# Layer 0's mixture: one spread gate for all row blocks, gate products on GpSimd, a token-major down-projection

## The reference, cut to what matters

```
scores = softmax(xf @ w_router.T)                 # 8 experts
expert_weights, expert_indices = top_k(scores, 2)
h = silu(einsum('td,edh->eth', xf, w1)) * einsum('td,edh->eth', xf, w3)
y = einsum('eth,ehd->etd', h, w2)
out = sum over the two chosen experts of expert_weights * y
```

## Time and profile before

| | |
|---|---|
| median of 3 runs | 1944.31 us (1942.88 to 1944.59) |
| the profiled execution | 1944.38 us, its span 1942.6 us |
| TensorE, matmuls | 1829.6 us busy, 94% |
| TensorE, weight loads | 1357.4 us, 70% |
| VectorE (DVE) | 1313.6 us, 68% |
| ScalarE (ACT) | 1128.7 us, 58% |
| GpSimd (POOL) | 1164.2 us, 60% |

### The profile page before, as it was taken

How to read it: one execution, slowest core, us unless ns; L and a number is a source line. 1 busy time by engine, 2 the same in 40 slices (tenths; PEclk the granted TensorE clock), 3 DMA queues, 4 the chain that set the end, 5 groups by cost and what they waited for, 6 DMA issues and landing times.

```text
span 1942.6 us, 32012 instructions
## 1 busy us (share of the span) xinstructions
PE 1829.6 (94%) x10178; PEld 1357.4 (70%) x10178; DVE 1313.6 (68%) x4504; ACT 1128.7 (58%) x2734; POOL 1164.2 (60%) x1702
## 2 busy tenths in 40 slices
PE   5999999998999999999999999999998999898987
PEld 3767777665666666566666667777788976796864
DVE  5964465788688777878688656435657655768673
ACT  5342344565685777667876786446445556435455
POOL 5420002479889888988898884126438655555554
PEclk9999999999999999999999999999999999899989
DMA  8000000001000000000000000000000011000001
GB/s 282 12 12 1 1 1 1 1 1 44 1 1 1 1 1 1 1 1 1 1 1 1 1 9 5 1 1 8 2 3 1 1 30 31 2 2 1 2 12 55
DMA packets 26492, 26.00 MB, mean 13 GB/s; under 512 B 3108, under 2 KB 23724, under 8 KB 25940
## 3 DMA queue, kind: packets, MB, share of 16 engines
q1 hardware_dynamic: 26324, 23.95, 4.0%
HBM read 21.80 MB, written 2.15 MB: 12 GB/s over the span
## 4 chain that ended last, share of the span: by engine, by line
PE 66%; POOL 16%; DVE 7%; ACT 6%; issue 4%; DMA 0%; POOLq 0%; SPq 0%; ACTq 0%; DVEq 0%
PE ps L86 60%; POOL arena L103 14%; PE ps L89 6%; ACT arena L97 5%; DVE arena L103 3%; ACT L97 1%; POOL arena L106 1%; DVE arena L106 1%; DVE arena L126 1%; DVE arena L109 1%; DVE arena L123 1%; DVE arena L141 1%; DMA rows<-in_rows 0%; DVE arena L129 0%; DVE arena L112 0%
## 5 line engine op out<-in xcount | busy, mean ns | idle before, releaser
L103 POOL TENSOR_TENSOR arena<-arena 128x128 f32<-128x128 f32 (+6 forms) x708 | 623.3, 891 | 298.0 <-DVE arena L109 158.6
L97 ACT ACTIVATE arena<-ps 128x128 f32<-128x128 f32 (+10 forms) x1100 | 363.3, 365 | 422.3 <-PE ps L86 305.8
L86 PE MATMUL ps<-arena 128*128 128x128 f32 (+4 forms) x2864 | 466.3, 298 | 27.1 <-DVE arena L103 12.6
L86 PEld LDWEIGHTS ps<-arena 128*128 128x128 f32 x2864 | 386.2, 194 | 125.0 <-issue 60.6
L103 DVE TENSOR_TENSOR arena<-ps,arena 128x128 f32<-128x128 f32 (+4 forms) x672 | 295.5, 450 | 173.7 <-PE ps L86 158.0
L86 PE MATMUL ps<-arena,moe 128*128 128x256 f32 (+1 forms) x1312 | 384.6, 433 | 0.7 <-DVE arena L103 0.4
L97 ACT ACTIVATE arena<-arena 128x128 f32<-128x128 f32 (+2 forms) x772 | 299.2, 438 | 59.1 <-POOL arena L103 46.1
L97 ACT ACTIVATE arena<-ps,cols 128x512 f32<-128x512 f32 x324 | 218.2, 689 | 170.0 <-PE ps L86 156.1
L86 PE MATMUL ps<-arena,cst 128*128 128x360 f32 (+1 forms) x768 | 295.5, 497 | 10.2 <-POOL arena L103 6.2
L86 PEld LDWEIGHTS ps<-arena,moe 128*128 128x128 f32 x1312 | 238.6, 192 | 69.6 <-issue 34.2
L89 PE MATMUL ps<-cst,arena 128*128 128x128 f32 (+2 forms) x1420 | 252.7, 280 | 33.2 <-ACT arena L97 17.1
(11 more groups left out here) (110 smaller groups left out, 2094.6 us busy)
## 6 DMA issues: line engine op xcount, KB each, us to landing
rows<-in_rows SPq DMA_DIRECT2D x1, 2253.0 KB, 9.2
moe<-in_L_ffn_w SPq DMA_DIRECT2D x3, 704.0 KB, 9.9
arena<-in_x SPq DMA_DIRECT2D x4, 512.0 KB, 9.0
wf<-in_wf SPq DMA_DIRECT2D x2, 1024.0 KB, 10.2
arena<-in_L_ffn_W SPq DMA_DIRECT2D x8, 256.0 KB, 3.0
out_dram<-arena SPq DMA_DIRECT2D x4, 512.0 KB, 3.2
wmod<-in_wmod SPq DMA_DIRECT2D x4, 384.0 KB, 8.8
arena<-kept SPq DMA_DIRECT2D x8, 192.0 KB, 3.0
```

Of the source, the lines that this page charges most:

```text
L86: return UNSENT if self.e is None else self.e.matmul(out, lhsT, rhs, start=start, stop=stop)
L97: return self.e.activation(out, in_, func, bias=bias, scale=scale)
L103: return UNSENT if self.e is None else self.e.tensor_tensor(out, a, c, op)
```

## The change

The units get another order: block j (of 11) holds units 16 j to 16 j + 15 of every expert, so every block has the same pattern of experts, partition p belonging to expert p // 16. `sel` shrinks to 24 x 128, and one product with it gives gates that fit all 11 blocks. The gate chain runs once for all 8 tiles. `ms` is taken twice per element (512 tokens each) and copied to SBUF by ScalarE (`gb`). The product with the gates moves to GpSimd (`mgated`). SiLU and product work in place in `hid`. `m2` has a 128-token slice of `hid` stationary and `w2` moving, 22 products a group, so its output is token-major: no `moT`, no `mo`; DVE multiplies it by the gain row, GpSimd adds it to x. The gain row of layer 0 is loaded into the place of layer 1's, which is loaded once an element's GpSimd has left the mixture. The weights are laid out on the host. All four strings of `TURNS` are new from the first hundred digits to the last.

```diff
@@ class Moe0
-        self.xn, self.hT = r.take(256), r.take(256)
-        self.hid = r.take(self.nb * 256)
-        self.sl = r.take(512)
...
+        self.hT, self.hid, self.gb = r.take(1024), r.take(self.nb * 256), r.take(1024)
+        self.xn, self.gTb = self.hid[:, 0:1024], self.hid[:, 2304:2816].bitcast(BF16)
...
@@ def moe0_pe(b)
+            for h in range(2):
+                ps = banks.take(pe, b, b, "mx", h)
...
+            for t in range(NT):
+                pe.wait_ge(*at("mh", b, t // 4))
+                ins = pe.mm(ps[:, 8 * t:8 * t + 8], m.hT[:, 128 * t:128 * t + 128], wsm("wr0"))
+            ins.then_inc(*pe.up(b, "mr", b))
+            yield
             for g in range(4):
...
-                    ps = banks.take(pe, b, b, "ms", l, g, j)
-                    pe.wait_ge(*at("mgT", b, l, g))
-                    for i in range(n):
-                        ins = pe.mm(ps[:, 256 * i:256 * i + 256], sel[:, col4(j + i)], m.gTb[0:24, :])
-                    ins.then_inc(*pe.up(b, "ms", b, l, g, j))
...
+                    if g == 0 and j == 4:
+                        yield
+                        ps = banks.take(pe, b, b, "mg")
...
+                        for t in range(NT):
+                            ins = pe.tr(pb[:, 128 * t:128 * t + 128],
+                                        m.g24[:, t, :, :].rearrange("p k e -> p (k e)"), ibf)
+                        ins.then_inc(*pe.up(b, "mg", b))
+                    if g == 0 and j == 6:
+                        for h in range(2):
...
+                            pe.mm(ps[:, :], sel[:, :], m.gTb[0:24, 512 * h:512 * h + 512]).then_inc(
+                                *pe.up(b, "ms", b, h))
...
-                pe.wait_ge(*at("mhid", b, l, g))
-                for j in range(m.nb):
-                    ins = pe.mm(ps[:, 0:256], w2[:, j, :], m.hid[:, 256 * j:256 * j + 256], start=(j == 0),
-                                stop=(j == m.nb - 1))
-                ins.then_inc(*pe.up(b, "m2", b, l, g))
...
-                for i in range(2):
-                    ins = pe.tr(ps[:, col4(i)], m.xn[:, col4(i)], ident)
-                ins.then_inc(*pe.up(b, "mo", b, l, g))
+                pe.wait_ge(*at("mgated", b, g))
                 for i in range(2):
+                    for j in range(m.nb):
+                        at_hid = 256 * j + 128 * i
+                        ins = pe.mm(ps[:, col4(i)], m.hid[:, at_hid:at_hid + 128], w2[:, j, :], start=(j == 0),
+                                    stop=(j == m.nb - 1))
+                ins.then_inc(*pe.up(b, "m2", b, g))
...
@@ def moe0_act(b)
+                    act.wait_ge(*at("m1", b, g, j))
+                    if g:
+                        act.wait_ge(*at("m2", b, g - 1))
+                    act.act(m.part(j, n), ps[:, 0:256 * n], ACT.Silu).then_inc(
+                        *act.up(b, "m1x", b, g, j, free=(b, "m1", g, j)))
...
+                            act.act(m.gb[:, 512 * h:512 * h + 512], ps[:, :]).then_inc(
+                                *act.up(b, "mgb", b, h, free=(b, "ms", h)))
...
@@ def moe0_dve(b)
-                    dve.tt(hj, hj, ps[:, 0:256 * n], ALU.mult).then_inc(*dve.up(b, "mhid", b, l, g, free=(b, "ms", l, g, j)))
...
+                dve.tt(four(m.group(g)), four(ps[:, 0:256]), over(r.row(5), 2), ALU.mult).then_inc(
+                    *dve.up(b, "my", b, g, free=(b, "m2", g)))
...
@@ def moe0_pool(b)
+                for j, n in moe_pairs(m.nb):
+                    yield
+                    hj = m.part(j, n).rearrange("p (j t) -> p j t", t=256)
+                    pool.wait_ge(*at("mgb", b, g // 2))
+                    pool.wait_ge(*at("mprod", b, g, j))
+                    pool.tt(hj, hj, over(m.gb[:, 256 * g:256 * g + 256], n), ALU.mult).then_inc(
+                        *pool.up(b, "mgated", b, g))
+                yield
+                xg = r.x[:, 2 * g:2 * g + 2, :]
+                pool.wait_ge(*at("my", b, g))
+                pool.tt(xg, xg, four(m.group(g)), ALU.add).then_inc(*pool.up(b))
...
@@ def queue_first(), SyncE
+            load("m1", moe0[0], A["w1f0"])
+            load("m3", moe0[1], A["w3f0"])
+            load("m2", moe0[2], A["w2f0"])
+            for b in range(B):
+                spread(f"gain0_{b}", b, 0, 5, 6)
...
                 queue_rows(b, 1, "l0", "dve")
-                spread(f"gain1_{b}", b, 1, 5, 6)
             queue_mods(2)
             queue_mods(3)
+            for b in range(B):
+                queue_gain(b, 1, ("moe", 0))
             queue_moe1()
...
@@ def constants()
-    sel = (r[:, None] == (np.arange(1408)[None, :] // 176)) * np.uint16(0x3F80)
+    sel = (r[:, None] == (i[None, :] // 16)) * np.uint16(0x3F80)
```

More of the change, by code:

```diff
@@ new lines, in moe0_pe @@
+            w2 = four(moe0[2])
+            enter(pe, b, "l0")
+            for h in range(2):
+                ps = banks.take(pe, b, b, "mx", h)
+                pe.wait_ge(*at("mn", b, h))
+                for i in range(4):
+                    ins = pe.tr(ps[:, col4(i)], m.tile(4 * h + i), ident)
+                ins.then_inc(*pe.up(b, "mx", b, h))
+                yield
+            ps = banks.take(pe, b, b, "mr")
+            for t in range(NT):
+                pe.wait_ge(*at("mh", b, t // 4))
+                ins = pe.mm(ps[:, 8 * t:8 * t + 8], m.hT[:, 128 * t:128 * t + 128], wsm("wr0"))
@@ new lines, in moe0_act @@
+            enter(act, b, "l0")
+            for h in range(2):
+                act.wait_ge(*at("mstats", b, h))
+                for t in range(4 * h, 4 * h + 4):
+                    norm_act(b, m.tile(t), r.x[:, t, :], t, "mn", b, h)
+                yield
+            for h in range(2):
+                ps = banks.get(b, "mx", h)
+                act.wait_ge(*at("mx", b, h))
+                act.act(m.hT[:, 512 * h:512 * h + 512], ps[:, :], scale=mcol(0, 4, b), bias=mcol(0, 3, b)).then_inc(
+                    *act.up(b, "mh", b, h, free=(b, "mx", h)))
+                yield
@@ new lines, in moe0_act @@
+                    act.act(m.part(j, n), ps[:, 0:256 * n], ACT.Silu).then_inc(
+                        *act.up(b, "m1x", b, g, j, free=(b, "m1", g, j)))
+                    if g == 0 and j == 2:
+                        yield
+                        act.wait_ge(*at("mshift", b))
+                        act.act(m.pr, m.pr, ACT.Exp).then_inc(*act.up(b, "mexp", b))
+                    if g == 0 and j == 4:
+                        yield
+                        ps = banks.get(b, "mg")
+                        act.wait_ge(*at("mg", b))
+                        act.act(m.gTb[0:24, :], ps[0:24, :].bitcast(BF16)).then_inc(
+                            *act.up(b, "mgT", b, free=(b, "mg")))
@@ L977, in moe0_dve @@
+                    if g == 0 and j == 6:
+                        for h in range(2):
+                            yield
+                            ps = banks.get(b, "ms", h)
+                            act.wait_ge(*at("ms", b, h))
+                            act.act(m.gb[:, 512 * h:512 * h + 512], ps[:, :]).then_inc(
+                                *act.up(b, "mgb", b, h, free=(b, "ms", h)))
+                yield
+            leave(act, b, ("moe", 0))
         def moe0_dve(b):
-            l, after = 0, "l0"
@@ L979, in moe0_dve @@
             m, r = Moe0(room[b]), room[b]
-            enter(dve, b, after)
-            yield from stats(b, [(r.x[:, t, :], t) for t in range(NT)])
-            yield from scales(b, "mstats", b, l)
+            enter(dve, b, "l0")
+            for h in range(2):
+                yield from stats(b, [(r.x[:, t, :], t) for t in range(4 * h, 4 * h + 4)])
+                yield from scales(b, "mstats", b, h)
+            yield
+            ps = banks.get(b, "mr")
+            dve.wait_ge(*at("mr", b))
@@ new lines, in moe0_dve @@
+            dve.cp(m.lg, ps[:, 0:64].rearrange("p (t e) -> p t e", e=8)).then_inc(*dve.up(b, free=(b, "mr")))
+            yield
+            dve.wait_ge(*dve.last(b))
+            for t in range(NT):
+                dve.max8(m.mx[:, t, :], m.lg[:, t, :]).then_inc(*dve.up(b))
+            yield
+            dve.wait_ge(*dve.last(b))
+            dve.tt(m.pr, m.lg, m.mx[:, :, 0:1].broadcast_to([128, NT, 8]), ALU.subtract).then_inc(
+                *dve.up(b, "mshift", b))
+            for t in range(NT):
+                dve.max_index(m.ix[:, t, :].bitcast(U32), m.mx[:, t, :], m.lg[:, t, :]).then_inc(*dve.up(b))
@@ L1053, in moe0_dve @@
[L1053 to L1059 removed]
+                for j, n in moe_pairs(m.nb):
+                    yield
+                    ps = banks.get(b, "m3", g, j)
+                    dve.wait_ge(*at("m3", b, g, j))
+                    dve.wait_ge(*at("m1x", b, g, j))
+                    dve.tt(m.part(j, n), ps[:, 0:256 * n], m.part(j, n), ALU.mult).then_inc(
+                        *dve.up(b, "mprod", b, g, j, free=(b, "m3", g, j)))
```

463 lines of the change are left out of this document (182 added, 281 removed).

## The result

The changed kernel takes 1882.45 us (median of 4 runs, 1881.73 to 1883.93) where the kernel before, run beside it, takes 1944.45 (1942.88 to 1946.16): a ratio of 0.9682, 95% interval 0.9665 to 0.9699, 62 us less. The forecast was 1905 us with a range from 1889 to 1931. The direction was right, the time lies 7 us outside the range.

The account below looks back on a forecast made before the run. The prediction took TensorE as the bound, losing time to streaming and to changes between expert and gate products. Its terms, -39.2 - 5 + 5 = -39 us from about 1944 us, gave 1905 us, range 1889 to 1931.

Parts of the forecast that it names:

- Order: Term for the rewritten order of all four engines to the kernel's end: taken as 0, with 10 us to either side.
- GpSimd and VectorE: Term for gate products moved to GpSimd: +5 us, 3 in the overlap with layer 1 and 2 elsewhere; bounds 0 and 35.
- TensorE in the mixture: Term for TensorE's work in the first mixture: fewer gate products, visits and transposes, slightly dearer down-projection; -39.2 us.
- only columns: Rival: in the first mixture only streamed columns are saved, mode-change time returning as bank waits; -18 us, 1926 us, chance 0.12.
- Start: Term for idle and half-clock TensorE at the first mixture's start: -5 us, between 0 and 9.75 us to gain.
- larger gain: Rival: the mixture's whole start is won, and the waits before `sel` too; 1894 us, chance 0.12.
- GpSimd takes over: Rival: 35 us of new GpSimd work lengthens the overlap with layer 1, if GpSimd exceeds 95% there; 1940 us, chance 0.10.
- slower by the new order: Rival: the new order of layer 1's attention leaves TensorE emptier; 1953 us at 5.5 points less, chance 0.05.
- signs of what would show it: Expected in the trace: eight `sel` products, long expert runs, no half clock near 85 us, busier GpSimd, mixture ending near 400 us.

Follow-up runs that it names:

- s2: The kernel before up to the end of its first mixture, then the changed kernel's written order on all four engines; 1941.37 us, ratio 0.9981.
- s1: The changed kernel up to 400 us, then the written order of the kernel before on all four engines; 1899.19 us, ratio 0.9754.
- r3: The kernel before with the same instructions and its order sought anew from beginning to end; 1927.46 us, ratio 0.9906.
- r4: The changed kernel with its order sought anew from beginning to end; 1870.71 us, ratio 0.9613 to the kernel before.
- r1: The kernel before with the same instructions, order sought anew only up to the end of layer 0's mixture; 1936.55 us, ratio 0.9956.
- u0: The changed kernel with its order sought anew only up to the end of layer 0's mixture, as control; 1886.38 us, ratio 0.9693.
- x1: The kernel before with its gate products on `sel` taking 128 rows, the added ones zero, instead of 24; 1932.77 us, ratio 0.9932.
- u2: The changed kernel with the old down-projection put back and the mixture's order sought anew; 1884.90 us, ratio 0.9685.
- u1: The changed kernel with the gate products back on VectorE and the mixture's order sought anew; 1888.34 us, ratio 0.9703.
- x2: The kernel before with the new unit layout and one `sel` product per group, copied by ScalarE, in the old written order; 1933.93 us, ratio 0.9937.
- r2: The kernel before with one `sel` product per group and the order sought anew up to the mixture's end; 1915.11 us, ratio 0.9841.

## Why the prediction was wrong, step by step

**The step that failed is "Order".** It said: "No row prices that. I take 0 and keep 10 us to either side." Measured, the order behind the mixture alone is worth 9.3 us (s2) to 10.8 us (s1), with the same instructions. Added to the measured 1882 us, they give an estimate of 1892 to 1893 us without the new order, inside the range. It is no accident of one trace: all six tails in the old order are longer than all six in the new one.

The sum was off by 23 us, and this step is not all of it. Behind the mixture 13 us came out where 0 stood. In the mixture 49 came out where 39 stood, and these 10 are terms of the waits: the start, idle time and half clock, brought 11.6 and not 5, the 5 charged for GpSimd and VectorE were not due, and TensorE's own work fell by 3 less than forecast. All three are worked out below.

What order is worth over the whole kernel the runs leave open. The order of before leaves 17.5 us on the table (spans of before and r3). Take r3 for a kernel of before with an order as good as after's (the tails are alike to 0.7 us, 1421.4 and 1422.1), and the 61.8 us between the spans are 44.3 of structure (1925.1 - 1880.8), for which -39 stood in the sum, and 17.5 of order. But after's own order leaves 15.4 us too (spans of after and r4), and with both sought anew the structure is worth 59.7 us by spans, 56.8 by medians; 12.5 of these lie in the tail, where TensorE's instructions are the same. By the heads alone the structure is worth 52.4 us (before to after), 47.2 (r3 to r4) or 40.0 (r1 to u0). I leave the choice open.

The sign could not be had from the trace of before, but an upper size could. The span and mean granted clock of core 0, of before and of after:

```profile
core 0: 1942.6 us, clock 0.983
```
```profile
core 0: 1880.8 us, clock 0.995
```

1.7% of 1942.6 us are 33 us of full-clock time lost in the kernel before, a quantity that a rewritten order moves; in the changed kernel it is about 10. "10 us to either side" was a number without a row.

**TensorE in the mixture, forecast -39.2: nearly right.** By the aligned records, TensorE's streaming in the first mixture went from 263.3 to 244.9 us, -18.4; the columns-only part of the sum was -18. What remains besides idle time and half clock, the changes of mode and other small losses between instructions, went from 34.3 to about 16.3 us, -18, against about -21. Together -36.4. With 6.5 us less idle time, 5.1 less half clock and 1.0 less of layer 1's work in the stage these are the 49 us. The rival "only columns" is refuted by that and by x1's timeline. The down-projection in the forms from 150 to 300 us of the changed kernel, beside the expert matmuls:

```profile
L86 PE MATMUL ps<-arena,moe 128*128 128x256 f32 x389 | 89.7, 382 | 0.0
...
L86 PE MATMUL ps<-moe,arena 128*128 128x128 f32 x440 | 50.7, 276 | 0.0
```

No wait before either, as taken from layer 1. u2 has the old down-projection and the same time as its control.

**Start, forecast -5, bounds 0 and -9.75: too small.** The hole is closed: 82 to 87 us has PE at 5.00 of 5 and 87 to 92 us a clock of 1.00. A smaller one is left, PE at 4.07 of 5 in 87 to 92 us, and the clock dips once, to 0.76 in 107 to 112 us. Half clock in the mixture went from 6.8 to 1.7 us and idle time from 10.0 to 3.6, together -11.6. The bound of -9.75 had 2.5 us for each of the two stretches at half clock, which lost 3.4 each, and the idle time of the first 73 us only; the rest of the idle time was left to the rival "larger gain", which had 16 us for all of this. The measured 11.6 lie between.

**GpSimd and VectorE, forecast +5: not due.** GpSimd is at 86.28 of 95 us in the overlap, 91%, fuller than the 86% forecast, and TensorE at 93.51, 98%, where it was 97% with a GpSimd at 55%. So nothing in the stage shows the 5 us. The durations were right, in the groups by form from 77 to 395 us:

```profile
L103 DVE TENSOR_TENSOR arena<-ps,arena 128x512 f32<-128x512 f32 x80 | 54.8, 689 | 63.5 <-PE ps L86 57.4 <-ACT arena L97 6.0
L103 POOL TENSOR_TENSOR arena<-arena 128x512 f32<-128x512 f32 x96 | 120.8, 1273 | 34.8 <-DVE arena L103 34.0 <-PE ps L89 0.2
...
L103 POOL TENSOR_TENSOR arena<-arena 128x256 f32<-128x256 f32 x31 | 22.5, 728 | 29.1 <-DVE arena L103 29.0
...
L103 DVE TENSOR_TENSOR arena<-arena 128x64 f32<-128x64 f32 x24 | 5.8, 256 | 4.7 <-ACT arena L97 4.4
```

VectorE's product from PSUM keeps its 689 ns beside a busy GpSimd. The prediction took its "the trace agrees" from the 689 ns before 309 us, where GpSimd was nearly idle; that row could not tell, this one can. The small steps of the gate chain cost 256 ns each, 5.8 us in all, inside their cover. The rival "GpSimd takes over" fails at its own condition, 95%, and u1 shows that the move neither wins nor loses more than a search is off: TensorE's 318 us bound the mixture with either engine.

**The rival "slower by the new order"** had the mechanism that carried the time out of the range, with the sign turned round: behind the mixture TensorE's idle time fell from 81.6 to 77.6 us and its busy time, for the same instructions, from 1417.4 to 1408.4.

**The forecast signs of what would show it** came true: `sel` x8, expert matmuls without gate products between them, no half clock near 85 us, GpSimd 113 us busier against about 120 (1164.2 to 1277.5), the mixture's end near 400 us (395.4). For the part behind the mixture they said only that layer 1 should not end where it did, and gave it no time.

**What stays open.** How the 9 to 11 us of the tail divide into clock and waits. How much an order of its own would bring x1 (for x2 that is r2). Why r4's tail is 12.5 us shorter than r3's, both sought the same way. And the best order of either kernel: the search is local, and u0 shows that it can end 4 us above an order that exists.

## What to carry to other kernels

Where the order of the turns is written out by hand, it is a part of the kernel with a price of its own: put the new strings on the old instructions, or seek both anew, before a gain is put down to the instructions. A change that frees the engine that binds may be paid only in part in an order made for the slower one: here the shared gate product brought 10 us in the old order and 21 in its own. And count columns and visits apart: a visit of 24-row products between products of 128 rows cost 0.30 us on top of its columns.

## What the runs showed of the hardware

- A visit of two bf16 products with 24 rows between fp32 products with 128 rows cost 0.30 us on top of their columns, 0.10 in the visit and 0.20 in the run behind it; with the same columns over 128 rows neither was left (the earlier trace rows and x1).
- In the tail of the kernel before, 2.7 and 3.4 idle us in 10 were followed by 10 and 17 us at 1.2 GHz. How much is lost so depends on the order: 20.8 us before, 4.7 in r4, for the same instructions of TensorE.
- GpSimd at 91% over 95 us did not hold back TensorE, at 98%, with three other elements to choose from. Nor does a half idle GpSimd fill TensorE: in x2 TensorE stood at 84% beside a GpSimd at 41%.
